# Adding the causal mask in PSUM on VectorE and halving wide score tiles, in the first attention of a two-layer kernel

## What is computed

```python
scores = jnp.einsum('bqd,bkd->bqk', Qr, Kr) / jnp.sqrt(jnp.float32(d))
mask = jnp.tril(jnp.ones((T, T), dtype=bool), k=1)
scores = jnp.where(mask[None, :, :], scores, -jnp.inf)
attn = jax.nn.softmax(scores, axis=-1)
out = jnp.einsum('bqk,bkd->bqd', attn, V)
...
x = x + _layernorm(_L0_attn_ref(_layernorm(x, axis=-1), L0_attn_Wq, L0_attn_Wk, L0_attn_Wv), axis=-1)
```

## Time and profile before

| | us |
|---|---|
| median of 3 runs (720.46 to 721.01) | 720.94 |
| the profiled execution | 720.41 |
| its span, first to last instruction | 718.5 |
| TensorE busy, share of the span | 641.9, 89% |
| VectorE busy | 534.9, 74% |
| ScalarE busy | 476.3, 66% |
| GpSimd busy | 183.3, 26% |

### The profile page before, as it was taken

How to read it: one execution, slowest core, us unless ns; L and a number is a source line. 1 busy time by engine, 2 the same in 40 slices (tenths; PEclk the granted TensorE clock), 3 DMA queues, 4 the chain that set the end, 5 groups by cost and what they waited for, 6 DMA issues and landing times.

```text
span 718.5 us, 9392 instructions
## 1 busy us (share of the span) xinstructions
PE 641.9 (89%) x3336; PEld 275.6 (38%) x3336; DVE 534.9 (74%) x1011; ACT 476.3 (66%) x471; POOL 183.3 (26%) x240
## 2 busy tenths in 40 slices
PE   8998899999999989889988888897898777999986
PEld 4575545455454513223222121122231111465555
DVE  6788430607336289999899999999999998686656
ACT  1344423333424399999999999998999899354221
POOL 5721100211102031491148101606500023040002
PEclk9999999999999999999999999999999999999999
DMA  9000200000404401135013520111101122400431
GB/s 316 13 1 1 91 1 0 1 1 7 125 1 117 125 1 56 56 86 142 16 56 99 144 55 25 33 56 56 55 14 42 56 53 67 118 0 1 135 132 29
DMA packets 32318, 42.77 MB, mean 60 GB/s; under 512 B 5264, under 2 KB 19344, under 8 KB 31888
## 3 DMA queue, kind: packets, MB, share of 16 engines
q1 hardware_dynamic: 32272, 42.18, 20.2%
HBM read 31.60 MB, written 10.55 MB: 59 GB/s over the span
## 4 chain that ended last, share of the span: by engine, by line
PE 41%; ACT 23%; DVE 23%; issue 11%; POOL 1%; DMA 1%; SPq 0%; DVEq 0%; POOLq 0%; ACTq 0%
ACT w_hh L1030 18%; PE ps L719 8%; PE ps L729 8%; DVE hid L1346 5%; DVE hid L1341 5%; PE ps L754 4%; PE ps L701 4%; PE ps L631 3%; PE ps L612 2%; PE ps L685 2%; PE ps L763 2%; DVE st L1132 2%; ACT probs L1001 2%; PE ps L542 1%; PE ps L465 1%
## 5 line engine op out<-in xcount | busy, mean ns | idle before, releaser
L1030 ACT ACTIVATE w_hh<-hid 128x2048 f32<-128x2048 f32 x128 | 249.8, 1951 | 8.5 <-DVE hid L1346 8.0
L631 PE MATMUL ps<-w_hh,v_h 128*32 128x512 f32 x1024 | 137.2, 607 | 33.6 <-ACT w_hh L1030 32.4
L1341 DVE TENSOR_TENSOR hid<-ps,probs 128x1024 f32<-128x1024 f32 x86 | 104.7, 1217 | 19.3 <-ACT probs L1001 16.1
L612 PE MATMUL ps<-q_s,k_s 64*128 64x512 bf16 x256 | 98.9, 387 | 15.4 <-DVE hid L1341 14.8
L1346 DVE SCALAR_TENSOR_TENSOR hid<-ps,probs 128x1024 f32<-128x1024 f32 x86 | 104.8, 1218 | 4.4 <-PE ps L612 3.3
L612 PE MATMUL ps<-q_w,k_w 64*128 64x512 bf16 x256 | 99.0, 387 | 0.0
L1001 ACT ACTIVATE probs<-ps 128x1024 f32<-128x1024 f32 x86 | 91.1, 1060 | 1.9 <-PE ps L612 1.9
L612 PE MATMUL ps<-q_g,k_s 128*128 128x512 bf16 x256 | 77.9, 386 | 1.1 <-ACT qkv_a L1001 1.1
L612 PEld LDWEIGHTS ps<-q_w,k_w 64*128 64x128 bf16 x256 | 23.7, 92 | 106.7 <-issue 53.6
L1685 POOL TENSOR_SCALAR rs<-mv 128x4 f32<-128x4 f32 x24 | 6.5, 273 | 199.2 <-DVE mv L1135 199.1
L729 PE MATMUL ps<-hid,w_hh 128*128 128x512 f32 x128 | 56.3, 592 | 0.0
(11 more groups left out here) (302 smaller groups left out, 1003.6 us busy)
## 6 DMA issues: line engine op xcount, KB each, us to landing
qk_rows<-part SPq DMA_DIRECT2D x48, 128.0 KB, 2.4
w_hh<-w_rows SPq DMA_DIRECT2D x4, 1024.0 KB, 9.8
qk_rows<-part_g SPq DMA_DIRECT2D x24, 128.0 KB, 2.4
q_g<-qk_rows SPq DMA_DIRECT2D x32, 96.0 KB, 2.2
k_s<-qk_rows SPq DMA_DIRECT2D x32, 96.0 KB, 2.2
q_s<-qk_rows SPq DMA_DIRECT2D x32, 96.0 KB, 2.4
k_w<-qk_rows SPq DMA_DIRECT2D x32, 96.0 KB, 2.5
q_w<-qk_rows SPq DMA_DIRECT2D x32, 96.0 KB, 2.4
```

Of the source, the lines that this page charges most:

```text
L612: last = mm(ps[:, base + half, :], k_op[rows, u, keys], q_op[rows, u, half * CHUNK:(half + 1) * CHUNK], start=True, stop=True)
L631: last = mm(ps[VW * g4:VW * g4 + VW, 6, :], v_h[:, u, mt, :], ee[:, mt % 2, g4 * CHUNK:(g4 + 1) * CHUNK], start=(mt == 0), stop=(mt == BT ...
L1030: A(ee[:, mt % 2, :], zz[:, mt % 2, :], ACT.Exp).then_inc(S["e"], 1)
L1341: v.tensor_tensor(zz[:, mt % 2, 0:SEQ], banks[:, 2 * CHUNK:4 * CHUNK], gg[s % 3], ALU.add).then_inc(S["z1"], 1)
```

## The change

The identity product with the mask goes, and with it the bfloat16 identity and its load. In its place VectorE adds the mask to the last w - 128 i columns of the scores, in place in PSUM, before the maximum that covers them. Of tiles with i of 4 or more (8 of the 16), the maximum and the exponential are taken in two pieces, of the first 512 columns and of the rest. Each piece has its own semaphore step: the first maximum waits only for the first bank's scores, and the transposes of the first 4 blocks only for the first exponential. The two maxima meet in the scaling instruction, the two row sums in an addition ahead of the reciprocal.

```diff
+        mx_1, rsum_1 = tiny[:, 0:TILES], tiny[:, TILES:2 * TILES]
...
+        def pieces(t):
+
+            return 2 if t % BT >= CT else 1
+
+        def pieces_to(t):
+            return sum(pieces(u) for u in range(t + 1))
...
-            sp.dma_start(ident_bf[:], ident_bf_in).then_inc(ld["con"], 16)
...
                 if t >= 2:
-                    pe.wait_ge(S["e_a"], t - 1)
+                    pe.wait_ge(S["e_a"], pieces_to(t - 2))
                 w = att_width(i)
                 for n0 in range(0, w, CHUNK):
                     n1 = min(w, n0 + CHUNK)
-                    m0, m1 = max(n0, P * i), n1
-                    bank = base + n0 // CHUNK
-                    masked = m1 > m0
-                    last = mm(ps[:, bank, 0:n1 - n0], q_t[:, b, i * P:(i + 1) * P], k_t[:, b, n0:n1],
-                              start=True, stop=not masked)
-                    if masked:
-                        last = mm(ps[:, bank, m0 - n0:m1 - n0], ident_bf[:],
-                                  mask[:, m0 - P * i:m1 - P * i], start=False, stop=True)
+                    last = mm(ps[:, base + n0 // CHUNK, 0:n1 - n0], q_t[:, b, i * P:(i + 1) * P], k_t[:, b, n0:n1],
+                              start=True, stop=True)
+                    if n0 == 0 and pieces(t) == 2:
+                        last.then_inc(S["s_a"], 1)
                 last.then_inc(S["s_a"], 1)
 
             def a_turn(t):
                 i = t % BT
-                pe.wait_ge(S["e_a"], t + 1)
+                pe.wait_ge(S["e_a"], pieces_to(t) - pieces(t) + 1)
...
                 for j in range(i + 1):
+                    if j == CT:
+                        pe.wait_ge(S["e_a"], pieces_to(t))
...
-                A(probs[:, t % 2, 0:w], banks[:, base:base + w], ACT.Exp, bias=nmx[:, t:t + 1],
-                  scale=ATT_SCALE, accum_out=rsum[:, t:t + 1]).then_inc(S["e_a"], 1)
+                for i, total in enumerate((rsum, rsum_1)[0:pieces(t)]):
+                    n0, n1 = i * CHUNK, w if i == pieces(t) - 1 else CHUNK
+                    A(probs[:, t % 2, n0:n1], banks[:, base + n0:base + n1], ACT.Exp, bias=nmx[:, t:t + 1],
+                      scale=ATT_SCALE, accum_out=total[:, t:t + 1]).then_inc(S["e_a"], 1)
...
             def a_max(t):
                 w = att_width(t % BT)
-                dve.wait_ge(S["s_a"], t + 1)
                 base = 2 * CHUNK * (t % 2)
-                me.step(v.tensor_reduce(mx[:, t:t + 1], banks[:, base:base + w], AX.X, ALU.max))
-                v.tensor_scalar(nmx[:, t:t + 1], mx[:, t:t + 1], -ATT_SCALE, None, ALU.mult).then_inc(S["m_a"], 1)
+                if pieces(t) == 2:
+                    dve.wait_ge(S["s_a"], pieces_to(t) - 1)
+                    me.mark(v.tensor_reduce(mx_1[:, t:t + 1], banks[:, base:base + CHUNK], AX.X, ALU.max))
+                n0 = CHUNK * (pieces(t) - 1)
+                dve.wait_ge(S["s_a"], pieces_to(t))
+                if t == 0:
+                    dve.wait_ge(ld["con"], 16)
+                seen = banks[:, base + P * (t % BT):base + w]
+                me.step(v.tensor_tensor(seen, seen, mask[:, 0:w - P * (t % BT)], ALU.add))
+                me.step(v.tensor_reduce(mx[:, t:t + 1], banks[:, base + n0:base + w], AX.X, ALU.max))
+                if pieces(t) == 2:
+                    v.tensor_scalar(nmx[:, t:t + 1], mx[:, t:t + 1], mx_1[:, t:t + 1], -ATT_SCALE,
+                                    ALU.max, ALU.mult).then_inc(S["m_a"], 1)
+                else:
+                    v.tensor_scalar(nmx[:, t:t + 1], mx[:, t:t + 1], -ATT_SCALE, None, ALU.mult).then_inc(S["m_a"], 1)
 
             def a_next(t):
 
-                dve.wait_ge(S["e_a"], t + 1)
+                dve.wait_ge(S["e_a"], pieces_to(t))
...
+                if pieces(t) == 2:
+                    me.step(v.tensor_tensor(rsum[:, t:t + 1], rsum[:, t:t + 1], rsum_1[:, t:t + 1], ALU.add))
                 me.step(v.reciprocal(rinv[:, t:t + 1], rsum[:, t:t + 1]))
```

More of the change, by code:

```diff
@@ L139, in sandwich @@
 def sandwich(nc, x_in, a_w, rope, b_w12, b_h1, b_h2, b_w3, b_s, b_s3, c_w, c_wo, c_bo, small,
-             d_wg, d_wu, d_wd, d_wr, ident_in, ident_bf_in, mask_in, before_in, out):
+             d_wg, d_wu, d_wd, d_wr, ident_in, mask_in, before_in, out):
     with ExitStack() as ctx:
@@ L156, in sandwich @@
         ident = sb("ident", [P, P])
-        ident_bf = sb("ident_bf", [P, P], BF16)
         mask = sb("mask", [P, P + 1], BF16)
@@ L501, in a_scores @@
                 if t == 0:
-                    pe.wait_ge(ld["con"], 32)
                     pe.wait_ge(S["rq2"], CHUNKS)
@@ L1929 @@
         "d_wd": f["L1_ffn_Wd"].transpose(1, 0, 2), "d_wr": f["L1_ffn_Wr"], "ident": eye,
-        "ident_bf": eye.astype(ml_dtypes.bfloat16), "mask": mask, "before": before,
+        "mask": mask, "before": before,
     }
```

## The result

The changed kernel takes 723.73 us (median of 7 runs, 722.98 to 725.79), the kernel before 720.46 beside it (719.80 to 721.23). The ratio is 1.0044, with a 95% interval of 1.0034 to 1.0055: 3.2 us slower (2.4 to 4.0).

A forecast was written before the change was run, and what follows sets the result against it. The attention was taken as bound by a serial chain through VectorE's maxima, ScalarE and TensorE. Its terms summed to +2.30 us on 720.41, 722.7, plus 0.5 for the runs' median: 723.2, range 721.8 to 725.0.

The forecast's parts named there:

- The price of an addition, 0.30 and 0.03: VectorE's mask addition in each tile: 0.30 us plus 0.03 for the wait behind it, 0.33 for a narrow tile.
- the sum: Delays added link by link along the attention's chain, from 0 up to 39.83 us to 2.30 us at the last result.
- If the second piece begins when that read ends: Wide tiles' split exponential on ScalarE: second piece after the first's accumulator read, at 0.78 us; net gain 0.09 per tile.
- the forecast's path: Chain through maxima 5, 7, 10, 11, 12 and 15 to the last result, with 2.30 us added in all.
- 0.44 less 0.36: Split exponential: four transposes done early, 0.44 us, against a last piece ready 0.36 later; net gain put at 0.09.
- Up to 39.83: 0 ... if each still arrives within the same memset: Tiles 0 to 4, before maximum 5: additions cost 0, taken up by scalings held by memsets; tile 1's margin 0.09 us.
- slips past the memset: Rival: tile 1's scaling arrives after 36.05, is held to about 37.9, and costs 1.2 us more, 724.4; chance 0.13.
- maximum 5 at 40.5 or later: Sign that the forecast is wrong: tile 5's maximum, expected near 39.8 us, starts late because tile 1's scaling is held.
- Faster, the additions fit into VectorE's idle time: Rival: 7.5 us of additions and other extra VectorE work fit into 10.5 us idle, giving 719.4 us; chance 0.04.
- No change to be measured: Rival: second exponential starts 0.19 us earlier, four times, and the rsum step hides (-0.38): 1.2 slower, 722.1; chance 0.12.

The follow-up runs named there:

- tile3_product: The changed kernel, but tile 3 keeps its mask as a product on TensorE: ratio 1.0023 to the kernel before, 722.72 us, attention 52.18 us.
- pair without holds: The kernel before and the changed kernel, each with the five memsets moved behind the roots of the norms: 719.59 and 721.77 us, attention 48.78 and 51.06.
- short_memsets: The changed kernel with the five memsets written through a float32 view, half as many elements: ratio 1.0014 to the kernel before, 721.47 us.
- split_alone: The changed kernel with all masks as products on TensorE, so only the cut into two pieces remains: ratio 0.9998 to the kernel before, 720.93 us.
- load_kept: The changed kernel with the load of the bfloat16 identity kept, though nothing reads it: ratio 1.0050 to the kernel before, 724.52 us.
- mask_alone: The changed kernel with all tiles whole, so only the mask addition on VectorE remains: ratio 1.0035 to the kernel before, 723.02 us.
- tile3_add_only: The kernel before with only tile 3's mask added by VectorE, nothing cut: ratio 1.0006 to the kernel before, attention 50.99 us.

## Why the prediction was right, and where it was off

The direction and the main mechanism held: VectorE's additions lie on the chain and are paid at tiles 7, 10, 11, 12 and 15 as forecast, and once more ahead of tile 7. One step failed, the one ahead of 39.83, and it cost 0.9 to 1.1 us. Step by step:

- *The price of an addition, 0.30 and 0.03.* Held. The groups by shape of the changed kernel, and the scaling that now takes two operands:

```profile
L1207 DVE TENSOR_TENSOR ps<-ps,mask 128x129 f32<-128x129 f32 x14 | 4.1, 295 | 1.5 <-PE ps L517 1.3
...
L1210 DVE TENSOR_SCALAR nmx<-mx,tiny 128x1 f32<-128x1 f32 x8 | 1.7, 214 | 0.3
...
L1213 DVE TENSOR_SCALAR nmx<-mx 128x1 f32<-128x1 f32 x8 | 1.2, 154 | 0.3
```

  The 0.295 is the 0.294 worked out from the 512-column row, so writing to PSUM in place added nothing that shows here. With its wait it is 0.33 (L1207 at 58.31, L1208 at 58.64). The recorded rows, 46.05 to 46.09, give 0.04 for the wait, where the sum took 0.03. Missed was the scaling: 0.214 where it takes the second maximum as an operand, against 0.154, so 0.06 for each wide tile.

- *"If the second piece begins when that read ends."* It begins 0.68 after the first, not 0.78, 0.09 into the accumulator's read. ScalarE in tile 4:

```profile
40.01 0.69 ACT L909 ACTIVATE probs<-ps,nmx 128x512 f32<-128x512 f32 x1 [1.71 <-DVE nmx L1210]
...
40.60 0.19 ACT L909 ACTIVATION_READ_ACCUMULATOR probs<-ps,nmx 128x1 f32 x1
40.69 0.36 ACT L909 ACTIVATE probs<-ps,nmx 128x129 f32<-128x129 f32 x1
...
40.94 0.20 ACT L909 ACTIVATION_READ_ACCUMULATOR probs<-ps,nmx 128x1 f32 x1
```

  That is the overlap of about 93 ns that the Trainium skill gives (ScalarE: Activation LUTs, What ACT_TABLE_LOAD costs), weighed in the prediction and not taken. The trace agrees with the page. Four times 0.1 are gained beyond the forecast, and the scaling takes four times 0.06 back; with both, the sum is 2.30 - 0.40 + 0.24 = 2.14, and tile3_product, which has the forecast's path and no slip, measured 2.14. That the two small errors nearly met is luck, and so is the closer 2.28 of the pair without holds, which comes to maximum 7 by another path. The recorded sum has small slips too: 0.44 less 0.36 is 0.08 and not 0.09 for each split, and its upper end adds up to 3.0, not 2.9.

- *"Up to 39.83: 0 ... if each still arrives within the same memset."* This is the step that failed: the term put at 0 was 0.94 to 1.08. The arrival was forecast to the hundredth: 0.09 ahead of the next memset in the sum, 0.08 in the trace. What was wrong is the criterion, that any time ahead of the next memset's row is enough: scalings were let in at 0.20 and more ahead and held at 0.08 and 0.09 (last section). The rival "slips past the memset" put the slip at an addition of 0.42 with its wait; it came at 0.33. Its price was put at 1.2 and its total at 724.4; measured are 0.94 to 1.08. Given 0.13, this rival was what happened on top of the forecast, in its mechanism, and its sign came: maximum 5 at 40.5 or later (40.72). The time held because the range reached over this rival, and it came within 0.5 of the 723.2 only because the kernel before was 0.5 faster beside it; by the difference, 3.2 lies outside the 1.9 to 2.9 of the sum.

- *Faster, the additions fit into VectorE's idle time.* Half of it did, which was not enough: VectorE's busy time in the stretch rose by 6.2 us and the stretch by 3.2. TensorE waits longer for the exponentials, 9.5 us in its row against 5.9 in 8 such waits before:

```profile
PE ps L532 <- ACT probs L909: 9.5, 10, 1.5
```

- *No change to be measured.* Of its two mechanisms one was half there (the second piece 0.1 earlier in place of 0.19), the other was not (L1222 stands in the chain ahead of maxima 7 and 15), and the slip outweighed them.

What I did not settle is why x's third chunk lands up to 1.3 us apart between executions of like kernels; the first product follows it one for one, so single executions move by up to four tenths of the change.

## What to carry to other kernels

Price an added instruction by where it lies on the chain, not by the engine's idle total: VectorE had 10.5 us idle in 50 and 6 uses of 0.33 still cost 2 us. Moving work off a busy TensorE pays only if the receiving engine isn't in the same serial chain; here the product cost 0.06 where the addition costs 0.33. Where an engine is held by another's long instructions, a small shift can cost a whole one of them, so shorten or move the long ones first: moving the memsets alone shortened the attention of the kernel before by 1.3 us; halved in length, they cost the changed one nothing any more.

## What the runs showed of the hardware that I had not expected

- A VectorE scaling held by a GpSimd memset is let go before the memset's row ends, so not for the whole row, as the prediction had it. A held one's end less the 0.29 it takes lies 0.21 ahead of q_s's end for tile 0 before, 0.21 ahead of k_w's end for tile 1 before, and 0.20 ahead of q_w's (38.43 - 0.29 against 38.34) with the change. The next memset's row starts some 0.06 before the last one's ends. So the next one would have to be beaten by about 0.15 us, not by 0. This fits every profile with such a meeting: let in when asked 0.20 (short_memsets), 0.41 (tile3_product) and 0.42 (before, and split_alone) ahead, held when asked 0.08 or 0.09 ahead (five profiles: the changed kernel twice, load_kept, mask_alone, tile3_add_only). The 0.15 is an inference from rows, not a run that swept it. A memset that lets VectorE in first is 0.08 longer in its row (1.88 against 1.80, 1.03 against 0.95).
- Setting the same bytes to zero through float32 takes 0.95 us where bfloat16 takes 1.80: GpSimd's memset goes by elements. Its float32 rows of 512, 1024 and 1792 elements take 0.52, 0.95 and 1.59 us, and bfloat16 of 2048 takes 1.80: about 0.1 us and 0.83 ns for each element.
